# Expert phase of an attention and expert kernel: rows routed already normalised, float32r first layer, root split between ScalarE and VectorE, stores one tile later

## The chip, the cores and the metric

The kernel runs on one core of a Trainium2 chip. The metric is the device time of one execution in microseconds (us). The kernel before has a median of 1305.73 us over three executions.

## The reference

`x` is (32, 256, 128) in float32: 8192 rows of 128. The first half normalises each row, runs causal attention with 16 heads of 64 through a low-rank key and value, projects, normalises and adds `x`. The second half normalises again and sends each row to one of 8 experts:

```python
def _sublayer(xs, g, b, W1e, b1e, W2e, b2e):
    mu = jnp.mean(xs, axis=-1, keepdims=True)
    var = jnp.mean(jnp.square(xs - mu), axis=-1, keepdims=True)
    h = (xs - mu) * jax.lax.rsqrt(var + EPS) * g + b
    return xs + jax.nn.relu(h @ W1e.T + b1e) @ W2e.T + b2e
feats = x.reshape(-1, x.shape[-1])          # x is the layer-normed row
expert = jnp.argmax(feats @ centroids.T, axis=1)
alpha = jax.nn.sigmoid(jnp.sum(feats * centroids[expert], axis=-1, keepdims=True))
out = alpha * y_of_that_expert + (1.0 - alpha) * feats
x = x + _layernorm(out, axis=-1)
```

W1 is 512x128 and W2 128x512 for each expert.

## The kernel before

**Engines.** Five instruction streams are written by hand: SP (loads), PE (TensorE), ACT (ScalarE), DVE (VectorE) and POOL (GpSimd). Each runs in the order written and waits on semaphores. A value that a float32r product needs exactly is kept in two parts: `cp` on ACT makes the upper part (line 720), a subtraction on DVE the rest (for instance `z_lo`, L910), and three products (low by high, high by low, high by high) are summed.

**Attention.** 32 blocks of 256 rows, eight slots to a block, one pair of heads to a slot; `phases` runs two blocks to a trip of its loop, then a last trip, then a drain of empty slots in which only the later stages of the pipeline still work. In a slot, POOL scales the probabilities of an earlier slot (L1144, the "norm"), and beside it carries the small work of the block before: x1 = x + normalised attention (L1092, into the row buffer `pay`), its statistics' root (L1104, L1105), the normalised row `fn` (L1068), and in slot 7 two scatters of 128 rows each into the DRAM table `routed_rows` (L1135), at places that DVE's `route` works out (`dst`, L955). A row there has 136 words: x1, its reciprocal root, its shift, a second root, the best score and the row's number.

**Drain.** After the last block's counts are known (`ends`, L958), ACT and SP each store four pads of 512 rows behind the experts' regions (`pad`, L230; each needs a number read from `ends`). PE works out W1 times beta for the bias (`first_bias`, L584), and ACT scales all of W1 by gamma in place (L780), in slot 7, after the pads. The last block's row goes through st2, `an` (L829), x1, st3, `fn`, scores, `dst` and the scatter. Then DVE makes the table of tiles (to L367), and the expert phase starts.

**Expert phase.** Tiles of 256 rows of one expert; 39 can be needed, and TILES is rounded up to 40. `ffn_phases` gives every engine eight unrolled slots, a loop of eight, and an end. In slot s, tile s is loaded (SP, L246), `ff` and `nn` are made from it (DVE, L373 and L381), turned (PE, L279) and copied to `nt` (ACT, L316); ACT also copies that expert's weights, 1029 columns, from `wx` to `wst` (L308) and takes the exponential for the gate (L311), which DVE finishes (L419, L428). Tile s-1 has its first layer (PE, L263, float32) and relu (ACT L323, DVE L390), tile s-2 its second layer (PE, L289, float32) and `yt` (ACT, L330), tile s-3 is turned back (PE, L272), joined with `ff` (L408) and measured (L414, L424) on DVE, and POOL takes the root (L446, L448). Tile s-4 is normalised (DVE, `on`, L399), added to its input (POOL, `res`, L442) and stored by two indirect DMAs (POOL, L452), whose descriptors POOL makes itself. POOL's slot before:

```python
pool.wait_ge(S["on_ready"], m + 1)
g.tensor_tensor(res[:, b], on[:], fin[:, sf, :, 0:P], ALU.add)
g.tensor_tensor(gve[:], gmv[:, b3, :, 1], eps_t[:], ALU.add)
g.tensor_tensor(grs[:, b3, :], gve[:], neg_half[:], ALU.pow)
for t in range(2):
    g.indirect_dma_start(out, ...)
```

**Start.** SP loads block 0 of x, the attention weights, then the expert weights (4.1 MB), and only then block 1 of x.

## Time and profile before

| | before |
|---|---|
| median of three executions | 1305.73 us (1304.86 to 1308.39) |
| the profiled execution | 1306.78 us, span 1305.0 us |
| PE busy | 1243.9 us (95%) |
| DVE busy | 1152.1 us (88%) |
| ACT busy | 1059.5 us (81%) |
| POOL busy | 923.5 us (71%) |
| mean granted TensorE clock | 0.975 |
| chain that ended last | PE 81%, DVE 9%, issue 4%, POOL 3% |
| largest DVE groups of the expert phase in that chain | `ff` 2%, relu 1%, `on` 1%, `gg` 1% |

The span is what the trace covers; the execution's own time is 1.8 us longer. The attention fills it to about 1082 us, the drain and the table take until about 1104 us, and the rest is the expert phase. A share of the whole span hides this, so the reading goes stage by stage. "Busy" of PE counts overlapping matmuls once; the distance from one matmul's start to the next is shorter than its listed length.

### The profile page before, as it was taken

The numbers are of one execution on the slowest core, as the hardware profiler recorded it, in microseconds if no ns is written. First come the engines' busy times: TensorE is split into PE (matmuls) and PEld (weight loads), VectorE is DVE, ScalarE is ACT, GpSimd is POOL, SyncE is SP. The second block draws the span as 40 slices with busy tenths as digits, with TensorE's granted clock in tenths as the row PEclk, the third lists the DMA queues.
The fourth block names the chain that finished last, engine by engine and source line by source line (L and its number), as shares of the span: only waits on it lengthen the run. The fifth ranks groups of instructions, "written<-read, shape, count | busy, mean of one in ns | idle before, by whom it ended". The sixth has DMA issues, their size and how long they took to land.

```text
span 1305.0 us, 40537 instructions
## 1 busy us (share of the span) xinstructions
PE 1243.9 (95%) x12200; PEld 1104.5 (85%) x12200; DVE 1152.1 (88%) x4556; ACT 1059.5 (81%) x3176; POOL 923.5 (71%) x1442
## 2 busy tenths in 40 slices
PE   6999999999999999999999999999999994999992
PEld 5889888989898888888988898888888884788782
DVE  4999999999999999999999999999999884799993
ACT  4998888888888888888888888888888872566661
POOL 3567777777777777777777777777777663488886
PEclk8999999999999999999999999999999996899996
DMA  5000000000000000000000000000000003121220
GB/s 221 6 10 14 12 12 12 12 12 12 12 12 12 12 12 12 12 12 12 12 12 12 12 12 12 12 12 12 12 8 9 11 10 93 41 63 58 60 60 5
DMA packets 38505, 31.90 MB, mean 24 GB/s; under 512 B 4882, under 2 KB 35734, under 8 KB 38080
## 3 DMA queue, kind: packets, MB, share of 16 engines
q1 hardware_dynamic: 31696, 21.47, 5.4%
q0 software_dynamic: 4656, 8.81, 2.0%
q10 hardware_dynamic: 2112, 1.11, 0.3%
q8 instruction: 21, 0.34, 0.1%
q14 instruction: 20, 0.16, 0.0%
HBM read 20.35 MB, written 12.07 MB: 25 GB/s over the span
## 4 chain that ended last, share of the span: by engine, by line
PE 81%; DVE 9%; issue 4%; POOL 3%; DMA 1%; ACT 1%; SPq 0%; POOLq 0%; DVEq 0%; ACTq 0%
PE psZU L659 17%; PE psS L594 14%; PE psZU L674 14%; PE psP L626 10%; PE psZU L662 7%; PE psT L608 5%; PE psT L609 4%; PE psT L610 4%; DVE ff L373 2%; DVE wup_s L390 1%; POOL out L452 1%; DMA xin<-x 1%; DVE on L399 1%; DVE gg L408 1%; PE psS L263 1%
## 5 line engine op out<-in xcount | busy, mean ns | idle before, releaser
L1144 POOL TENSOR_TENSOR prob<-prob,rinv 128x256 f32<-128x256 f32 (+1 forms) x512 | 412.5, 827 | 254.3 <-DVE rinv L905 253.6
L756 ACT ACTIVATE prob<-nscore,nmax 128x128 f32<-128x128 f32 (+1 forms) x1024 | 453.5, 450 | 6.2 <-DVE nmax L887 5.3
L887 DVE CUSTOM_DVE_ANT_0 nscore<-psS,mask 128x128 f32<-128x128 f32 (+1 forms) x1024 | 321.5, 351 | 2.5 <-PE psS L594 1.5
L896 DVE TENSOR_TENSOR p_lo<-psP,p_hi 128x768 fp32r<-128x768 f32 x256 | 243.6, 951 | 3.0 <-ACT p_hi L720 3.0
L720 ACT ACTIVATE t_hi<-psT 128x512 fp32r<-128x512 f32 x256 | 153.0, 598 | 111.3 <-PE psT L610 108.5
L875 DVE TENSOR_TENSOR t_lo<-psT,t_hi 128x512 fp32r<-128x512 f32 x256 | 176.0, 687 | 70.5 <-ACT t_hi L720 70.1
L720 ACT ACTIVATE p_hi<-psP 128x768 fp32r<-128x768 f32 x256 | 206.7, 808 | 3.5 <-PE psP L626 3.5
L756 ACT ACTIVATION_READ_ACCUMULATOR prob<-nscore,nmax 128x1 f32 x1024 | 199.3, 195 | 0.0
L910 DVE TENSOR_TENSOR z_lo<-psZU,z_hi 128x512 fp32r<-128x512 f32 x256 | 174.1, 680 | 8.6 <-ACT z_hi L720 3.1
L594 PE MATMUL psS<-t_hi,t_lo 64*128 64x128 f32 (+1 forms) x1024 | 164.6, 317 | 0.4 <-DVE nmax L887 0.4
L608 PE MATMUL psT<-xt_hi,qk_lo 128*128 128x256 f32 x512 | 155.1, 303 | 2.3 <-DVE t_lo L875 1.2
L626 PE MATMUL psP<-ident,prob 64*128 64x64 f32 x3072 | 151.0, 231 | 0.5 <-DVE p_lo L896 0.5
L720 ACT ACTIVATE z_hi<-psZU 128x512 fp32r<-128x512 f32 x256 | 148.5, 580 | 2.1 <-PE psZU L662 2.1
L674 PE MATMUL psZU<-z_hi,b_lo 128*128 128x256 f32 x512 | 145.6, 284 | 0.0
L626 PEld LDWEIGHTS psP<-ident,prob 64*128 64x128 f32 x3072 | 116.0, 139 | 34.0 <-issue 0.7
L609 PE MATMUL psT<-xt_lo,qk_hi 128*128 128x256 f32 x512 | 143.2, 280 | 0.0
L674 PE MATMUL psZU<-z_hi,b_hi 128*128 128x256 f32 x512 | 143.2, 280 | 0.0
L594 PE MATMUL psS<-t_lo,t_hi 64*128 64x128 f32 (+1 forms) x1024 | 143.2, 275 | 0.0
L594 PE MATMUL psS<-t_hi 64*128 64x128 f32 (+1 forms) x1024 | 142.9, 275 | 0.0
L610 PE MATMUL psT<-xt_hi,qk_hi 128*128 128x256 f32 x512 | 142.9, 279 | 0.0
L674 PE MATMUL psZU<-z_lo,b_hi 128*128 128x256 f32 x512 | 142.7, 279 | 0.0
L659 PE MATMUL psZU<-p_hi,xk_lo 128*128 128x512 f32 x256 | 126.8, 495 | 1.3 <-DVE z_lo L910 1.2
(175 smaller groups left out, 3268.2 us busy)
## 6 DMA issues: line engine op xcount, KB each, us to landing
fin<-routed_rows SPq DMA_DIRECT2D x40, 136.0 KB
wx<-ffn_w SPq DMA_DIRECT2D x2, 2058.0 KB, 12.5
xin<-x SPq DMA_DIRECT2D x32, 128.0 KB, 2.2
xres<-x SPq DMA_DIRECT2D x32, 128.0 KB, 2.1
out<-res,fin POOLq DMA_INDIRECT x80
routed_rows<-padr ACTq DMA_DIRECT2D x4, 272.0 KB, 5.1
routed_rows<-padr SPq DMA_DIRECT2D x4, 272.0 KB, 4.4
wup_s<-wup SPq DMA_DIRECT2D x1, 1024.0 KB, 5.8
```

The source lines that it names most:

```text
L594: last = mm(psS[:, e, a:z], qq[h, tb, 0, q * P:(q + 1) * P], kk[h, tb, 1, 0:z - a], start=(n == 0), stop=(n == 2))
L608: mm(psT[:, m, :], qk_lo[:, r, m, :], xt_hi[:, db, :], start=True, stop=False)
L609: mm(psT[:, m, :], qk_hi[:, r, m, :], xt_lo[:, db, :], start=False, stop=False)
L610: last = mm(psT[:, m, :], qk_hi[:, r, m, :], xt_hi[:, db, :], start=False, stop=True)
L626: last = nc.tensor.transpose(psP[:, e, 64 * n:64 * n + 64], prob[half, s % 4, h, k * P:(k + 1) * P], ident[half, half])
L659: mm(psZ[:, :, :], xx[:, zx, 0, :], pp[:, zb, :, 0:T], start=(n == 0), stop=False, skip_group_check=True)
L674: last = mm(psU[:, 0:T], bb[:, hh, :], zz[:, ub, h, :], start=(ur == 0 and h == 0 and n == 0), stop=(ur == PAIRS - 1 and h == 1 and n == 2))
L720: cp = lambda o, i: nc.scalar.activation(o, i, ACT.Copy)
L756: last = nc.scalar.activation(prob[:, pb, h, a:z], nscore[:, (s - lag) % 2, h, a:z], ACT.Exp, bias=nmax[:, pb, h, q:q + 1], scale=-1.0, ac ...
L887: last = v.tensor_tensor_reduce(nscore[:, n1, h, a:z], psS[:, h, a:z], mask[:, a:z], -1.0, -MASKED, ALU.add, ALU.min, nmax[:, p1, h, q:q + 1])
L896: v.tensor_tensor(by_half(p_lo, s % 2), psPh, by_half(p_hi, s % 2).bitcast(F32), ALU.subtract).then_inc(S["p_split"], 1)
L1144: last = g.tensor_tensor(pr, pr, rinv[:, p2, :, q:q + 1].broadcast_to([P, 2, z - a]), ALU.mult)
```

## The change

- The routed row has 260 words: the row normalised twice (128), x1 (128), the gain alpha times the second root, the second root squared times EPS, and the number. POOL and DVE make these in the attention's slots (POOL slots 4, 5 and 7; ACT and DVE slot 6 take exponential, sum and reciprocal for alpha). The scatter goes behind the norm in slot 7. The expert phase no longer makes `ff`, `nn` and alpha.
- W1 scaled by gamma is made in two parts in a buffer of its own, one expert in each of the drain's slots 1 to 8: ACT the upper part, DVE the rest. The eight scalings at the end are gone.
- The first layer is three float32r products per block of 128 (12 in place of 4 float32 ones, each of which is two instructions); `nt` has an upper part (ACT) and a rest (DVE). ACT copies the weights as 1024 and 517 columns.
- The second root: ACT takes Sqrt of two single columns with the row's own EPS as bias, DVE the reciprocal. POOL's two operations go; it copies the two row numbers instead.
- `gg` moves to s-4, `on` and `res` to s-5, the stores to s-6, behind `res` of the following tile; the load of a tile waits for `res` and not for the stores. TILES is 39, and buffers are shared with the attention's.
- SP loads block 1 of x ahead of the expert weights.

```diff
-    TILES += -TILES % 8
-        sp.wait_ge(stored[s], n0 + n0)
+        sp.wait_ge(S["res_ready"], m0 + s - 7)
+        sp.wait_ge(S["ids_ready"], m0 + s - 7)
 # PE, slot s
-        last = mm(psH[:, j, :], wst[:, (s - 1) % 4, j * P:(j + 1) * P], nt[:, (s - 1) % 2, :],
-                  start=True, stop=True)
+        for n, (m, nt) in enumerate(((1, nt_hi), (0, nt_lo), (0, nt_hi))):
+            last = mm(psH[:, j, :], w1st[:, b, m, j * P:(j + 1) * P], nt[:, b, :],
+                      start=(n == 0), stop=(n == 2))
 # ACT, slot s (new order: yt, root, first weights, relu, nt, second weights)
+        act.wait_ge(S["gmv_ready"], m0 + s - 4)
+        for t in range(2):
+            last = nc.scalar.activation(gsd[:, b, t:t + 1], gmv[:, b, t, 1:2], ACT.Sqrt,
+                                        bias=fin[:, sf, t, C_EPS:C_EPS + 1])
 # DVE, end of slot s
+        v.reciprocal(grs[:, b, :], gsd[:, b, :])
+        last = v.tensor_scalar(on[:, b, t, :], gg[:, b, t, :], gmv[:, b, t, 0:1], grs[:, b, t:t + 1], ...)
+        v.tensor_tensor(nt_lo[:, s % 2, :], psN[:, 0:T], nt_hi[:, s % 2, :].bitcast(F32), ALU.subtract)
 # POOL, slot s
-        g.tensor_tensor(gve[:], gmv[:, b3, :, 1], eps_t[:], ALU.add).then_inc(S["gve_done"], 1)
-        g.tensor_tensor(grs[:, b3, :], gve[:], neg_half[:], ALU.pow).then_inc(S["grs_ready"], 1)
+        g.tensor_copy(ids[:, c, :], fin[:, sf, :, C_ID].bitcast(U32)).then_inc(S["ids_ready"], 1)
 # ACT, attention's slots
+    if not live(0) and 1 <= s <= E:
+        nc.scalar.activation(w1[:, s - 1, 0, :], wx[:, s - 1, 0:FB * P], ACT.Copy, scale=gam[:, s - 1:s])
-    if not live(0) and s == 7:
-        act.wait_ge(S["bias_done"], E // 2 + 1)
-        for e in range(E):
-            last = nc.scalar.activation(wx[:, e, 0:FB * P], wx[:, e, 0:FB * P], ACT.Copy,
-                                        scale=gam[:, e:e + 1])
 # DVE, head of a slot
+    if not live(0) and 1 <= s <= E:
+        dve.wait_ge(S["w1_hi_done"], s)
+        v.scalar_tensor_tensor(w1[:, s - 1, 1, :], wx[:, s - 1, 0:FB * P], gam[:, s - 1:s],
+                               w1[:, s - 1, 0, :].bitcast(F32), ALU.mult, ALU.subtract)
 # DVE, end of slot 6
+    v.tensor_scalar(ea1[:], ea[:], 1.0, None, ALU.add)
+    v.reciprocal(alpha[:], ea1[:])
 # POOL, slot 4
+    g.tensor_tensor(pay[:, db, :, 0:P], fn[:], rstd2[:].unsqueeze(2).broadcast_to([P, 2, P]), ALU.mult)
 # SP, start
+    sp.wait_ge(S["x_loaded"], 16)
+    load_x(xin, 1, 1, S["x_loaded"])
     for dst_, src in ((cent[:], cent_t), ..., (wx[:, E // 2:], ffn_w[:, E // 2:])):
```

ACT in the drain, before: from the copy `at` of the last block to the exponential of the first tile.

```order
L720 ACTIVATE at<-psZU 128x256
L229 TENSOR_LOAD ends
L229 ISA x2
L230 ISA
L230 DMA routed_rows<-padr 128x4x136
...
L230 DMA routed_rows<-padr 128x4x136
L780 ACTIVATE wx<-wx,gam 128x512 x8
L720 ACTIVATE ft<-psM 128x256
```

The same place of the change (`w` is the new buffer of scaled W1, `best` the best score).

```order
L764 ACTIVATE w<-wx,gam 128x512 x2
L721 ACTIVATE at<-psZU 128x256
L781 ACTIVATE ea<-best 128x2
...
L237 DMA routed_rows<-padr 128x4x260
L764 ACTIVATE w<-wx,gam 128x512 x2
L721 ACTIVATE ft<-psM 128x256
```

Two of the eight scalings, experts 6 and 7, stand behind ACT's four pads. DVE at the same place of the change, from the destination of the block before the last to the statistics of the last block's x1:

```order
L955 TENSOR_REDUCE dst<-dsel 128x2
L958 CAST ends<-base 128x8
L1002 TENSOR_SCALAR ea<-ea 128x2
L1004 RECIPROCAL alpha<-ea 128x2
L964 SCALAR_TENSOR_TENSOR w<-wx,gam,w 128x512
L819 BN_STATS st<-psM 128x6 x2
L825 BN_AGGR mv<-st 128x2 x2
L964 SCALAR_TENSOR_TENSOR w<-wx,gam,w 128x512
L830 TENSOR_SCALAR an<-psM,mv,rs 128x128 x2
L971 TENSOR_TENSOR wx<-psT,wx 128x8x4
L819 BN_STATS st<-pay 128x6 x2
```

Before, `st<-psM` (L818) followed `ends` directly; now the rest of W1 for expert 6 stands between them. POOL in the expert phase's loop, before and then in the change (`wq_s` is where `res` now lies, `xres` where `on` lies, `softmax` where `fin` lies):

```order
L442 TENSOR_TENSOR res<-on,fin 128x256
L445 REGISTER_ALU
L446 TENSOR_TENSOR gve<-gmv,eps_t 128x2
L448 TENSOR_TENSOR grs<-gve,neg_half 128x2
L452 DMA out<-res,fin 8192x128 x2
```

```order
L446 TENSOR_TENSOR wq_s<-xres,softmax 128x256
L447 COPY ids<-softmax 128x2
L453 DMA out<-wq_s,ids 8192x128 x2
```

The root has left POOL; the stores that follow `res` are those of the tile before.

## Rows read from the trace of the kernel before

**Rows 1.** Busy time by window, attention: length, then PE, PEld, DVE, ACT, POOL, clock, DMA, GB/s.

```profile
600.00:604.00 4.00, 4.00 (x52) 3.60 (x50) 3.74 (x16) 3.47 (x11) 3.50 (x5) 1.00 0.05 17
```

**Rows 2.** Busy time by window, expert phase.

```profile
1140.00:1256.00 116.00, 112.32 (x549) 92.96 (x548) 112.80 (x469) 75.13 (x164) 99.33 (x139) 1.00 0.21 61
```

**Rows 3.** Timeline, one tile of the expert phase: start us, length us, engine, line.

```profile
1198.83 1.89 PE L263 MATMUL psS<-nt,wst 128*128 128x256 f32 x8
1201.03 0.20 PEld L279 LDWEIGHTS psZU<-ident,nn 128*128 128x128 f32 x2 [0.33 <-DVE nn L381]
...
1201.68 0.64 DVE L399 TENSOR_SCALAR on<-gg,gmv,grs 128x128 f32<-128x128 f32 x2
...
1202.59 0.97 POOL L452 DMA_INDIRECT out<-res,fin  x1 [0.30 <-DVE on L399]
...
1203.04 1.89 PE L263 MATMUL psS<-nt,wst 128*128 128x256 f32 x8
1203.23 0.46 DVE L419 TENSOR_SCALAR ea<-ea 128x2 f32<-128x2 f32 x1
...
1203.57 0.74 POOL L442 TENSOR_TENSOR res<-on,fin 128x256 f32<-128x256 f32 x1
...
1205.45 1.03 POOL L452 DMA_INDIRECT out<-res,fin  x1 [0.19 <-issue]
```

**Rows 4.** Chain of waits: start, length, what; matmuls as issued one behind another.

```profile
1118.25 1.73 PE psT L289 x8
```

**Rows 5.** Chain of waits, drain: float32r matmuls.

```profile
1073.21 0.71 PE psZU L674 x6
```

**Rows 6.** Groups by line, 1080 to 1305 us: busy us, mean ns, then idle before.

```profile
L308 ACT ACTIVATE wst<-wx 128x1029 f32 x40 | 42.5, 1063 | 21.8 <-issue 12.6 <-DVE table L367 8.4 <-ACT yt L330 0.8
...
L311 ACT ACTIVATE ea<-fin 128x2 f32<-128x2 f32 x40 | 7.6, 189 | 1.5 <-DMA fin<-routed_rows 1.5
```

**Rows 7.** Timeline, DVE before POOL has any store to issue.

```profile
1107.38 0.16 DVE L419 TENSOR_SCALAR ea<-ea 128x2 f32<-128x2 f32 x1
```

**Rows 8.** Timeline, start of the kernel.

```profile
0.78 1.28 ACT L720 ACT_TABLE_LOAD   x1 [0.65 <-PEq L1181]
...
20.79 0.49 DVE L818 BATCH_NORM_STATS2 st<-xin 128x6 f32<-128x128 f32 x2 [2.21 <-DMA xin<-x]
```

**Rows 9.** Timeline, attention, end of slot 6 on DVE and POOL.

```profile
632.01 0.66 DVE L910 TENSOR_TENSOR z_lo<-psZU,z_hi 128x512 fp32r<-128x512 f32 x1
...
632.18 1.61 POOL L1144 TENSOR_TENSOR prob<-prob,rinv 128x256 f32<-128x256 f32 x2 [0.69 <-DVE rinv L905]
```

**Rows 10.** Chain of waits, the following slot's product on PE.

```profile
633.85 0.90 PE psZU L659 x3
```

**Rows 11.** Timeline, drain, from the pads to the last block's destination.

```profile
1084.35 5.21 ACTq L230 DMA_DIRECT2D routed_rows<-padr  x4
...
1086.49 0.21 POOL L1011 TENSOR_TENSOR ve<-mv,eps_t 128x2 f32<-128x2 f32 x1
...
1088.41 0.72 POOL L1092 TENSOR_TENSOR pay<-an,xres 128x256 f32<-128x256 f32 x1 [0.84 <-DVE an L829]
...
1090.12 5.01 ACT L780 ACTIVATE wx<-wx,gam 128x512 f32<-128x512 f32 x8 [7.64 <-PE psT L584]
1090.23 0.47 DVE L818 BATCH_NORM_STATS2 st<-pay 128x6 f32<-128x128 f32 x2
...
1092.29 1.58 POOL L1068 TENSOR_SCALAR fn<-pay,mv 128x128 f32<-128x128 f32 x2 [0.19 <-POOL pay L1105]
...
1098.38 0.17 DVE L955 TENSOR_REDUCE dst<-dsel 128x2 uint32<-128x16 f32 x1
```

**Rows 12.** Timeline, expert phase: the first tile's first layer, the last tile's, the last store.

```profile
1108.69 3.78 PE L263 MATMUL psS<-nt,wst 128*128 128x256 f32 x8 [0.47 <-ACT nt L316]
...
1275.36 1.89 PE L263 MATMUL psS<-nt,wst 128*128 128x256 f32 x8
...
1295.75 0.97 POOL L452 DMA_INDIRECT out<-res,fin  x1 [0.30 <-issue]
```

319 lines of the change are left out of this document (171 added, 148 removed).

## The prediction, made before the changed kernel ran

> **What bounds the kernel now.** I read the busy time by window first, because the page's shares mix stages. In the attention PE is busy for 4.00 of 4.00 us [rows 1] and DVE for 3.74: PE is the bound, and what ACT, DVE or POOL gain or lose there costs nothing as long as PE's inputs stay early. In the expert phase PE is busy 112.3 of 116 us, DVE 112.8, POOL 99.3, ACT 75.1 [rows 2]. These hardly differ, so I went to the timeline of one tile [rows 3]. First layer to first layer is 1203.04 - 1198.83 = 4.21 us. In it PE waits 0.33 us for `nn`. Its own work is two layers of 1.73 us each [rows 4] and two pairs of transposes; these fill 4.21 - 0.33 - 3.46 = 0.42 us. So PE works 3.88 and idles 0.33. POOL has hardly a gap: `res` begins at 1203.57, the next store at 1205.45, so `res` and the root take 1.88 us; then come 1.03 us for the first store, a gap of 0.30 and 0.97 for the second, 4.18 together. POOL and PE meet at nearly the same period, with DVE between them. One can not gain without the others.
>
> **The start.** DVE waits 2.21 us for block 1 of x [rows 8], which stands in SP's queue behind 4.1 MB of expert weights, and everything after it in DVE's queue waits too, then POOL, then PE. Ahead of those weights the load is early. The weights are needed only in the drain, a thousand us later. Gain 2.2 us; bounds 1 and 3.5 (the next waiter may be 1 us behind; or PE loses less speed while it waits).
>
> **Attention.** Per block POOL gets a 128x256 product of about 0.75 us (like `res` [rows 3]) and four operations of about 0.2, and loses one; ACT one small Exp; DVE one addition (0.16 [rows 7]) and one reciprocal of about that. POOL's scatter now stands behind the norm. The place to check is the end of DVE's slot 6: `z_lo` ends at 632.67 [rows 9] and the product that needs it starts at 633.85 [rows 10], 1.18 us later. 0.3 us of DVE fit. I take 0; bounds 0 and the second rival.
>
> **The drain.** It looks as if 5.01 us of scaling by ACT left the path [rows 11]. They do little there: `ft` waits for them until about 1095.0 (1090.12 and 5.01, less an overlap of 0.1), and `fn`, its other input, starts at 1092.29 and with 1.58 us and the transposes would have let it start at 1094.6. Gain 0.4. What is added is worse. Two of the new scalings stand behind ACT's four pads, whose issue lasts from 1084.35 to 1089.56, and DVE takes the rest of W1 ahead of the last block's statistics. Forward: the DVE operations ahead of `dst` and `ends` move the pads by 0.5, to 1090.1. ACT's scaling 0.7 (5.01 / 8 and its end), to 1090.8. DVE's rest, a 128x512 operation like `z_lo` (0.66 [rows 9]), to 1091.5; statistics 0.5 and their aggregation 0.3, to 1092.3. From POOL's root to the end of x1 it takes 1089.13 - 1086.49 = 2.64, to 1095.0. The statistics of x1 now start at 1095.05, before at 1090.23 (where they waited for the bias, which PE finishes long before now). From there `fn` comes 2.06 later as before, and `dst` too: 4.8 late, less the 0.4 of `ft`, 4.4. Behind it the order is a little longer: the gain needs DVE's reciprocal after `dst`, a POOL product, then the scatter; and the table starts 0.3 later. About 0.4 of this shows in the first load. The pads carry 1040 bytes a row in place of 544, so they last longer, but they end near 1100 and the last scatter comes at 1104. The first tile's load carries twice the bytes (+0.3); it sheds `ff` and `nn` (-1.2) and gets `nt_lo` and a semaphore (+0.6). Sum: 4.4 + 0.4 - 0.3 = **+4.5 us** at the first product. Bounds +2 (if the two scalings get ahead of the pads' numbers) and +7 (if every link has a gap more).
>
> **A tile of the expert phase.** PE: six float32r products take 0.71 us [rows 5], so twelve take 1.42 where the float32 layer took 1.73; PE works 3.88 - 0.31 = 3.57. POOL loses the root and gets a copy of about 0.2: `res` 0.74, copy 0.2, gap 0.2, stores 2.30, that is 3.44. DVE loses four passes of 128x128 (two pairs like `on`, 0.64 each, a little less), the addition with its hold (0.46) and gets `nt_lo`, half of a `z_lo` with a fixed part, 0.42: 4.09 (112.8 over 27.6 tiles) - 1.2 - 0.46 + 0.42 + 0.1 = 2.95. ACT gets longer: 75.1 over 27.6 is 2.72; less the Exp 0.19, plus 512 columns more at 1.06 for 1029 [rows 6], 0.53, plus a fixed 0.1, plus two Sqrt like that Exp, 0.38: 3.54. The root is no longer a chain of POOL's, but ACT and DVE pass it to and fro; it has a whole slot for each step.
>
> So PE, ACT and POOL stand at 3.57, 3.54 and 3.44: no engine can wait long for another. The ring that closes each tile is first layer, relu, `nt` upper part, `nt` rest, first layer: 1.42, three ACT operations of 256 columns (two relus and the copy to `nt`; each below the 0.53 of 512 columns [rows 6], together 1.2 to 1.5) and 0.42, with four semaphores 3.2 to 3.5, and DVE has the reciprocal and `on` (0.64) between relu and `nt_lo`. It fits below 3.57 only when `on` isn't held. Today's interlock costs PE 0.33; I leave that as it is: **3.90 us** a tile. Bounds 3.57 (PE alone) and 4.15 (first rival).
>
> Does a store hold `on`? The small DVE addition takes 0.16 alone [rows 7] and 0.46 when it starts at 1203.23 inside a store; it ends with that store [rows 3]. So DVE is held by a store's later part. But `on` at 1201.68 took 0.64 for its pair inside the store before it, the twin of the one at 1205.45, with hardly any hold. The Trainium skill, SBUF — State Buffer, section Who interferes with whom, says that whoever issues first keeps the shared ports for the whole instruction and the other is blocked fully. By that rule `on` would wait for each store's end, which the addition bears out and `on` does not; this is the first rival, with its price from the rows.
>
> From the first tile's first layer to the last's the trace shows 1275.36 - 1108.69 = 166.7 us [rows 12] for 39 steps: 39 x 4.21 = 164.2 and 2.5 for slow first tiles. Now 38 steps (39 tiles): 38 x 3.90 = 148.2, the same 2.5, and one load of the table for Sqrt, 1.3 by the load of 1.28 at the start [rows 8]: 152.0. **-14.7 us**, of which 4.2 are the tile left out. The Trainium skill, ScalarE: Activation LUTs, section What ACT_TABLE_LOAD costs, adds a drain of 1.38 us to each load; the sum would be 1.4 worse by it, and no row here shows that drain.
>
> **The end.** From the last tile's first layer to the end of the last store it takes 1296.72 - 1275.36 = 21.4 us, at POOL's pace. The new lag is longer by a slot for `yt` and one for the stores; about six pairs of stores are left, 6 x 3.44 = 20.6, and some 2 of phase: 22.6. **+1.2**; bounds -1 and +3.
>
> **Sum.** -2.2 + 0 + 4.5 - 14.7 + 1.2 = -11.2 us. From the profiled execution's 1306.8 us that is 1295.6; that execution is 1.05 us above the median of the three shown, and against the median of 1305.73 it is **1294.5 us**.
>
> **Rivals.**
> 1. *The stores hold `on`.* Then `on` waits for the second store, `res` for `on`, and the next stores for `res`: 0.60 + 0.74 + 0.2 + 0.2 + 1.03 + 0.30 + 0.97 and 0.1 for semaphores, 4.15 us a tile. 38 x 0.25 = 9.5 more: 1304.0. For it speaks the held addition, against it the free `on`. A partial hold gives 4.05 and 1300.
> 2. *Slower: the new addition in DVE's slot 6 is held by the norm.* It stands right behind the reciprocal that releases POOL's norm of 1.61 us [rows 9]. If it starts after the norm, it waits for its end: 1.61 and 0.15, against the 1.18 us that `z_lo` has in hand, so PE stands still for 0.6 us in each of 31 blocks: +18, 1312.5. It decides from a hold of 1.5 us on: 0.5 a block costs the whole gain and 0.3% more. Against it: the norm starts at 632.18, after `z_lo` at 632.01, so the addition, in `z_lo`'s place, is first.
> 3. *The drain does not lengthen, or the tiles run at 3.7.* If ACT and DVE get the last scalings done in the shadow of other work, 4.5 falls to 0: 1290. At 3.7 us a tile it is 1287.
> 4. *The period stays at 4.2*, since ACT's copies come late for the relus: only the tile and the start are won, -2.2 + 4.5 - 2.9 + 1.2, so 1306.
>
> **How the numbers follow.** My forecast with periods between 3.75 and 4.0 (1289 to 1298.5) gets 0.53, the first rival 0.20, the second 0.06, the third 0.14, the fourth 0.07. A measurement of this kernel can tell about 0.3%, 3.9 us: below 1301.8 is faster. There lie the forecast, the third and half of the first, 0.77. The other half, the fourth and a little of the second are no change, 0.17; slower 0.06. The range, 1287 to 1303.5, leaves out the second and fourth rival and the worst of the first.
>
> **What would show it.** Right: no DVE wait for x at 20 us; first layer to first layer about 3.9 us; ACT and PE both near full in the phase, POOL waiting for `on`; the statistics of the last x1 near 1095 less the 2.2 won at the start, waiting behind the rest of W1 and so behind ACT's pads; one table load. Wrong: `on` pairs of 1 us or more that end with a store (first rival); PE waits for `z_lo` once a block (second); ACT without gaps and PE waiting for relu (fourth); statistics of x1 that start where they did (third).

## The result, and the profile after

The changed kernel is slower: 1346.65 us median of four runs (1345.34 to 1352.24) against 1307.06 us for the kernel before beside it, ratio 1.031, 95% interval 1.029 to 1.034. The forecast was 1294.5 us in a range of 1287 to 1303.5, so both the number and the side are wrong. The profiled execution took 1352.24 us with a span of 1348.0 us, 43.0 more than the span before. Cut at the same places in both timelines (first product of block 1 and of block 30, the first and the last tile's first layer):

| stretch | before, us | after, us | difference | forecast |
|---|---|---|---|---|
| to block 1 | 47.45 | 43.98 | -3.5 | -2.2 |
| block 1 to block 30 (29 blocks) | 948.2 | 982.5 | **+34.3** | 0 |
| block 30 to the first tile's first layer | 113.05 | 130.8 | **+17.8** | +4.5 |
| first tile to last tile | 166.7 | 160.0 | **-6.7** | -14.7 |
| last tile's first layer to the end of the span | 29.6 | 30.7 | +1.1 | +1.2 |

(The forecast counted the end to the end of the last store: 22.5 us against 21.4, +1.2.) Three terms failed: the attention, which I had costed at nothing, the drain, and the tiles.

**The attention.** The waits of 100 to 1000 us of the kernel after (engine, what it was about to write, line, releaser: us in total, times, longest). The last four lines shown have no counterpart of any size in the kernel before (the first of them has 2.2 us there, the others are not in its list):

```profile
...
ACT t_hi L721 <- PE psT L611: 101.0, 185, 0.9
DVE t_lo L876 <- ACT t_hi L721: 44.0, 106, 0.7
PEld psZU L660 <- issue: 38.2, 27, 1.5
DVE an L830 <- POOL rs L1024: 37.7, 27, 1.4
PE psZU L660 <- DVE z_lo L911: 33.5, 27, 1.3
ACT softmax L757 <- DVE nmax L888: 22.6, 26, 1.0
...
```

27 times in 900 us, at 33.9 us a block, is once a block. The timeline of one block, POOL, then DVE, then PE (start, length, engine, line, what, and in brackets the idle time before it):

```profile
619.05 1.61 POOL L1155 TENSOR_TENSOR softmax<-softmax,rinv 128x256 f32<-128x256 f32 x2 [2.27 <-DVE rinv L906]
620.84 1.12 POOL L1170 DMA_INDIRECT routed_rows<-pay,dst  x1 [0.17 <-issue]
622.26 0.96 POOL L1170 DMA_INDIRECT routed_rows<-pay,dst  x1 [0.30 <-issue]
623.25 0.21 POOL L1022 TENSOR_TENSOR ve<-mv,eps_t 128x2 f32<-128x2 f32 x1
623.53 0.72 POOL L1024 TENSOR_TENSOR rs<-ve,neg_half 128x2 f32<-128x2 f32 x1
...
624.29 0.73 DVE L830 TENSOR_SCALAR an<-psM,mv,rs 128x128 f32<-128x128 f32 x2 [1.40 <-POOL rs L1024]
624.94 0.68 DVE L911 TENSOR_TENSOR z_lo<-psZU,z_hi 128x512 fp32r<-128x512 f32 x1
...
625.77 0.47 PE L660 MATMUL psZU<-p_both,xk_lo 128*128 128x512 f32 x1 [1.24 <-DVE z_lo L911]
```

Read it upwards. PE waits 1.24 us for `z_lo`; `z_lo` stands in DVE's queue behind `an`, which waits 1.40 us for the root `rs`; and the root stands in POOL's queue behind the two scatters, which with their gaps take from 620.66 to 623.22. Ahead of its norm POOL now sits idle for 2.27 us: into that gap the scatter used to fall. The product that waits is that of [rows 10].

**The drain.** Timeline after, from `ends` to the last x1:

```profile
1127.25 0.16 DVE L958 CAST ends<-base 128x8 int32<-128x8 f32 x1
...
1133.61 1.33 ACT L764 ACTIVATE w<-wx,gam 128x512 fp32r<-128x512 f32 x2 [7.21 <-issue]
1134.37 0.75 DVE L964 SCALAR_TENSOR_TENSOR w<-wx,gam,w 128x512 fp32r<-128x512 f32 x1 [6.68 <-ACT w L764]
1135.04 0.49 DVE L819 BATCH_NORM_STATS2 st<-psM 128x6 f32<-128x128 f32 x2
...
1138.96 0.49 DVE L819 BATCH_NORM_STATS2 st<-pay 128x6 f32<-128x128 f32 x2 [0.74 <-POOL pay L1104]
```

Here the forecast holds: DVE waits 6.68 us for the two scalings that stand behind ACT's pads. From `ends` to the statistics of the last x1 it takes 11.7 us. Before it took 7.0, from the line below to 1090.23 [rows 11]:

```profile
1083.22 0.16 DVE L958 CAST ends<-base 128x8 int32<-128x8 f32 x1
```

So this part is 4.7 longer, where I had worked out 4.3 (4.8 for the statistics, of which 0.5 was the later `ends`). The other 13.2 us lie ahead of `ends`, where I had put 0.5.

**The tiles.** First and last first layer and the last store:

```profile
1157.27 0.58 PE L274 MATMUL psS<-xt_hi,p_both 128*128 128x256 f32 x1 [0.93 <-DVE xt_lo L432]
...
1317.27 0.39 PE L274 MATMUL psS<-xt_hi,p_both 128*128 128x256 f32 x1
...
1338.81 0.98 POOL L453 DMA_INDIRECT out<-wq_s,ids  x1 [0.30 <-issue]
```

160.0 us for 38 steps are 4.21 us a step, the pace of the kernel before [rows 3, 12] and not 3.90. The waits of 1185 to 1300 us:

```profile
PEld psS L274 <- DVE xt_lo L432: 17.2, 24, 1.4
...
PE psS L274 <- DVE xt_lo L432: 10.2, 15, 1.0
ACT xt_hi L345 <- PE psZU L290: 9.7, 12, 1.0
ACT wup_s L340 <- PE psS L274: 7.8, 12, 1.2
DVE xt_lo L432 <- ACT xt_hi L345: 6.7, 10, 0.7
```

(`xt_hi`, `xt_lo` are `nt_hi`, `nt_lo` here.) In the first experiment below, with the very same code in this phase, the third and the fifth of these lines are gone and the second is down to 0.7 us.

### The profile page after: what moved, and what is told of

It is laid out like the page before. It is cut to its first block, busy times and chain, and to the rows that moved or that the text cites. A ratio compares the mean times of both kernels' runs of the same rounds, so it can differ in the third digit from the quotient of the medians.

```text
span 1348.0 us, 40987 instructions
## 1 busy us (share of the span) xinstructions
PE 1234.4 (92%) x12336; PEld 1102.3 (82%) x12336; DVE 1132.3 (84%) x4455; ACT 1087.3 (81%) x3281; POOL 924.9 (69%) x1495
## 4 chain that ended last, share of the span: by engine, by line
PE 68%; issue 11%; POOL 9%; DVE 6%; DMA 2%; ACT 1%; ACTq 0%; POOLq 0%; DVEq 0%; SPq 0%
PE psZU L660 14%; PE psS L595 11%; PE psZU L675 11%; PE psP L627 8%; PE psZU L663 5%; PE psT L609 4%; PE psT L610 4%; PE psT L611 3%; PE psS L274 3%; POOL routed_rows L1170 3%; POOL softmax L1155 2%; POOL out L453 2%; DVE z_lo L911 2%; DMA xin<-x 1%; DVE softmax L888 1%
## 5 line engine op out<-in xcount | busy, mean ns | idle before, releaser
L1155 POOL TENSOR_TENSOR softmax<-softmax,rinv 128x256 f32<-128x256 f32 (+1 forms) x512 | 412.8, 827 | 257.0 <-DVE rinv L906 257.0
L757 ACT ACTIVATE softmax<-softmax,nmax 128x128 f32<-128x128 f32 (+1 forms) x1024 | 453.8, 450 | 31.9 <-DVE nmax L888 30.8
L888 DVE CUSTOM_DVE_ANT_0 softmax<-psS,mask 128x128 f32<-128x128 f32 (+1 forms) x1024 | 322.4, 353 | 4.9 <-issue 2.6
L897 DVE TENSOR_TENSOR p_both<-psP,p_both 128x768 fp32r<-128x768 f32 x256 | 243.9, 953 | 4.8 <-ACT p_both L721 4.8
L721 ACT ACTIVATE p_both<-psP 128x768 fp32r<-128x768 f32 x256 | 206.7, 807 | 5.3 <-PE psP L627 5.3
L757 ACT ACTIVATION_READ_ACCUMULATOR softmax<-softmax,nmax 128x1 f32 x1024 | 199.5, 195 | 0.0
L660 PE MATMUL psZU<-p_both,xk_lo 128*128 128x512 f32 x256 | 127.3, 497 | 40.0 <-DVE z_lo L911 40.0
L660 PE MATMUL psZU<-p_both,xk_hi 128*128 128x512 f32 x512 | 161.8, 397 | 0.0
L627 PE MATMUL psP<-ident,softmax 64*128 64x64 f32 x3072 | 151.8, 232 | 0.5 <-DVE p_both L897 0.5
L627 PEld LDWEIGHTS psP<-ident,softmax 64*128 64x128 f32 x3072 | 116.6, 139 | 34.3 <-issue 0.9
```

The lines of the kernel that those rows point to most:

```text
L627: last = nc.tensor.transpose(psP[:, e, 64 * n:64 * n + 64], prob[half, s % 4, h, k * P:(k + 1) * P], ident[half, half])
L660: mm(psZ[:, :, :], xx[:, zx, 0, :], pp[:, zb, :, 0:T], start=(n == 0), stop=False, skip_group_check=True)
L721: cp = lambda o, i: nc.scalar.activation(o, i, ACT.Copy)
L757: last = nc.scalar.activation(prob[:, pb, h, a:z], nscore[:, (s - lag) % 2, h, a:z], ACT.Exp, bias=nmax[:, pb, h, q:q + 1], scale=-1.0, ac ...
L888: last = v.tensor_tensor_reduce(nscore[:, n1, h, a:z], psS[:, h, a:z], mask[:, a:z], -1.0, -MASKED, ALU.add, ALU.min, nmax[:, p1, h, q:q + 1])
L897: v.tensor_tensor(by_half(p_lo, s % 2), psPh, by_half(p_hi, s % 2).bitcast(F32), ALU.subtract).then_inc(S["p_split"], 1)
```

## The experiments

Each is told by its edit against the kernel named. Experiments 1 to 4 ran together on one chip, and so did 5 to 8, 9 to 11, 12 to 14, and 15 and 16, each group on another chip and with the kernel before beside it. This matters for the pace of the tiles, as the part behind experiment 16 shows. "A step" is the mean distance of the tiles' first layers, first to last, over 38 steps.

**1. The scatter ahead of the norm.** The changed kernel with one block moved in POOL's slot 7:

```diff
                     g.tensor_tensor(pay[:, db, :, C_GAIN], rstd2[:], alpha[:], ALU.mult).then_inc(S["gain_ready"], 1)
+                if r == 7 and live_b(2):
...
+                    for t in range(2):
+                        g.indirect_dma_start(rows, bass.IndirectOffsetOnAxis(ap=dst[:, db, t:t + 1], axis=0),
+                                             pay[:, db, t, :], None).then_inc(S["rows_written"], 16)
                 if live(2):
...
-                if r == 7 and live_b(2):
...
-                    for t in range(2):
-                        g.indirect_dma_start(rows, bass.IndirectOffsetOnAxis(ap=dst[:, db, t:t + 1], axis=0),
-                                             pay[:, db, t, :], None).then_inc(S["rows_written"], 16)
```

> The changed kernel with one move: in POOL's slot 7 the scatter of the routed rows stands ahead of the norm again (behind the product that makes the gain), as in the kernel before; all else stays. Theory A (the place of the scatter): behind the norm it stands directly ahead of the root that DVE's `an` waits for, `z_lo` is queued behind `an`, and PE waits about 1.27 us in each steady block; with the move the block period falls from 34.00 us back to 32.7, some 27 blocks, and the stalls of 2.7 us at the start of the drain go too: the kernel comes to 1302 to 1312 us, 35 to 45 less than the changed kernel's 1346.65, and `an <- POOL rs` vanishes from the waits. Theory B (the operations that POOL, ACT and DVE gained in the attention are what is late, wherever the scatter stands): the period stays above 33.5 us and the kernel above 1335. Theory C (both): the period falls by part, 1318 to 1330.

Measured: 1297.14 us (1294.87 to 1299.3, four runs), ratio to before 0.992 (0.990 to 0.995), so 49.5 us less than the changed kernel. `an <- POOL rs` is gone from the waits, and 29 blocks take 947.5 us (before 948.2). POOL in one block:

```profile
597.19 1.12 POOL L1160 DMA_INDIRECT routed_rows<-pay,dst  x1 [0.97 <-POOL pay L1148]
598.61 0.96 POOL L1160 DMA_INDIRECT routed_rows<-pay,dst  x1 [0.30 <-issue]
599.59 1.62 POOL L1168 TENSOR_TENSOR softmax<-softmax,rinv 128x256 f32<-128x256 f32 x2
...
601.43 0.72 POOL L1024 TENSOR_TENSOR rs<-ve,neg_half 128x2 f32<-128x2 f32 x1
```

The root follows the norm at once; POOL's queue holds the same work, in another order. Theory A holds. That the gain is above the expected 35 to 45 comes from the tiles: a step takes 3.89 us, not 4.21, with not a line changed there, which is 12.2 us of the 49.5. Those 12.2 are not shown to be the scatter's: the two kernels ran on different chips.

**2. The kernel before with the scatter behind the norm.** The same move in the old kernel, nothing added:

```diff
-                if r == 7 and live_b(2):
...
-                        g.indirect_dma_start(rows, bass.IndirectOffsetOnAxis(ap=dst[:, db, t:t + 1], axis=0),
-                                             pay[:, db, t, :], None).then_inc(S["rows_written"], 16)
                 if live(2):
...
                     prep_rstd(b0 + db + 3)
+                if r == 7 and live_b(2):
...
+                        g.indirect_dma_start(rows, bass.IndirectOffsetOnAxis(ap=dst[:, db, t:t + 1], axis=0),
+                                             pay[:, db, t, :], None).then_inc(S["rows_written"], 16)
```

> The kernel before with that one move the other way: the scatter of slot 7 stands behind the norm and the preparation, ahead of the next slot's root; no operation is added. Theory A: 27 blocks x 1.27 us and the stall at the drain's start are added, 1340 to 1350 us. Theory B (the added operations): nothing happens, 1305 to 1309. Theory C (the scatter costs only together with the added operations of POOL): in between, 1315 to 1330.

Measured: 1347.79 us (1344.45 to 1353.55), ratio 1.033 (1.030 to 1.036). The move alone costs 41 us. It shows the same waits, `DVE an L829 <- POOL rs L1013: 35.9, 26, 1.4` among them. 29 blocks take 981.7 us (+33.5), and from block 30 to the first tile 119.4 us (+6.3). Since experiment 1 has all the added operations and the old length of a block, they cost nothing that shows; B and C fall.

**3. The scalings of W1 earlier as well.**

```diff
+        W1_AT = ((0, 1), (2,), (3,), (4, 5), (6,), (7,))
...
-                if not live(0) and 1 <= s <= E:
+                if not live(0) and s < 6:
                     act.wait_ge(S["ffnw_loaded"], 5 * 16)
-                    nc.scalar.activation(w1[:, s - 1, 0, :], wx[:, s - 1, 0:FB * P], ACT.Copy,
-                                         scale=gam[:, s - 1:s]).then_inc(S["w1_hi_done"], 1)
+                    for e in W1_AT[s]:
+                        nc.scalar.activation(w1[:, e, 0, :], wx[:, e, 0:FB * P], ACT.Copy,
+                                             scale=gam[:, e:e + 1]).then_inc(S["w1_hi_done"], 1)
...
-                if not live(0) and 1 <= s <= E:
+                if not live(0) and 1 <= s < 7:
+                    for e in W1_AT[s - 1]:
```

(The last two lines are DVE's, whose rests follow one slot later.)

> The kernel of the move above (scatter ahead of the norm) and a second edit: ACT scales the eight experts' W1 in the drain's slots 0 to 5 (two, one, one, two, one, one) in place of 1 to 8, DVE takes the rests one slot later, so that no scaling stands behind ACT's pads and no rest ahead of the last block's statistics waits for them. Theory (the prediction's drain term): the statistics of the last x1 come some 4.8 us earlier and the first tile with them: 4 to 5.5 us less than the run with the scatter alone. Rival (the drain is longer for another reason: the low clock of a PE that was held, or the longer order of scatter, pads and loads): 0 to 1 us less; or the two more scalings per slot make ACT late for PE in the drain's first slots: 1 to 3 us more.

Measured: 1289.82 us (1289.08 to 1294.53), ratio 0.988 (0.986 to 0.991), 7.3 us less than experiment 1. From `ends` to the last statistics it takes 7.2 us again (4.5 less). The rest was got ahead of `ends`: 94.6 us from block 30 in experiment 1, 90.7 here, 87.6 before. The windows show what differs there: PE's busy time and the granted clock (ninth number, the one before DMA's share), experiment 1, then experiment 3.

```profile
1061.00:1065.00 4.00, 2.31 (x24) 1.88 (x23) 3.58 (x11) 3.34 (x11) 3.92 (x6) 0.96 0.01 3
1065.00:1069.00 4.00, 4.00 (x28) 3.98 (x26) 2.57 (x8) 1.21 (x2) 2.70 (x5) 0.50 0.11 33
1069.00:1073.00 4.00, 4.00 (x23) 3.59 (x21) 1.66 (x3) 2.02 (x3) 3.50 (x9) 0.50 0.00 0
1073.00:1077.00 4.00, 4.00 (x24) 3.58 (x25) 1.50 (x2) 0.81 (x1) 1.23 (x5) 0.50 0.01 4
```

```profile
1062.00:1066.00 4.00, 2.37 (x25) 2.00 (x24) 3.66 (x12) 4.00 (x14) 3.90 (x6) 1.00 0.06 23
1066.00:1070.00 4.00, 3.49 (x34) 3.19 (x33) 4.00 (x8) 2.67 (x7) 2.30 (x3) 1.00 0.11 33
1070.00:1074.00 4.00, 4.00 (x40) 3.75 (x39) 3.29 (x7) 2.75 (x5) 2.91 (x7) 1.00 0.00 0
```

In the first, PE stands still for part of 4 us in the drain's second slot and then runs some 12 us at half its clock (1.2 GHz) with its queue full. In the other it pauses at least as long, but the clock stays at 1.00. In the changed kernel PE is busy 2.45 and 1.54 us in two such windows (1100 to 1108), and then the clock is 0.50 from 1108 to 1120 us. In its repeat (experiment 5) PE is busy 2.25 and 1.56 us in the same windows, and the clock is then 0.76 for 4 us and 1.00 for the next 8; `ends` comes 3.9 us sooner behind block 30. So the low clock goes with some 3.9 us, and it can differ between two executions of one kernel: the 3.9 us that experiment 3 gains ahead of `ends` are not shown to be the edit's, although all four executions of it have a higher mean clock (0.974 to 0.978) than those of experiment 1 (0.970 to 0.972).

**4. The early load of x alone.**

```diff
             sp.dma_start(wo_s[:], wo).then_inc(S["o_loaded"], 16)
+            sp.wait_ge(S["x_loaded"], 16)
+            load_x(xin, 1, 1, S["x_loaded"])
...
-            sp.wait_ge(S["x_loaded"], 16)
-            load_x(xin, 1, 1, S["x_loaded"])
```

> The kernel before with only the load of block 1 of x ahead of the expert weights. Theory: the whole gain of 3.5 us that the changed kernel shows up to the start of block 1 (first product of block 1 at 43.98 us in place of 47.45) comes from this: 3.3 to 3.7 us less, about 1303.4 us. Rival: it brings the 2.2 us of DVE's wait as predicted, and the rest is owed to another edit: 1304.8.

Measured: 1302.0 us, in a single execution. Block 1 starts at 42.55 us; block 0 itself takes 30.3 us from its first product on, as in the changed kernel, and 34.1 before. (The first product comes between 11.2 and 13.7 us in the different executions, so the block's own length is the better measure: -3.8.) The whole gain at the start is the load's.

**5. The changed kernel again.** From here on the question is the pace of the tiles.

> The changed kernel once more, unchanged, on the chip of the next runs. Its expert phase ran at 4.21 us a tile, and the same phase, behind the attention with the scatter moved, at 3.82; nothing in the phase differs between the two. Theory P (two paces: the phase settles into one or the other by the moment at which loads, stores and transposes meet, and the moment is set by what runs ahead of it): the pace is again 4.2, or it is 3.8 in this execution, and then the times of this kernel fall into two groups some 12 us apart, about 1340 and 1347 to 1352. Theory Q (the slow pace belongs to the kernel, through the order on POOL): 4.21 in the profile again, times 1345 to 1352. Theory R (one disturbed execution): 3.82 in the profile, times about 1346 as they were.

Measured: 1345.6 us (1344.2 to 1346.29), ratio 1.030 (1.028 to 1.032), a step 4.18 us; from block 30 to `ends` 96.9 us in this execution, against 100.8 in the first. The slow pace is repeated. R falls; so does P's second group of times.

**6. Half the bytes in each load.** The row's layout becomes normalised values, gain, eps, number, x:

```diff
-                sp.dma_start(fin[:, s], rows[bass.ds(row, T), :].rearrange("(t p) c -> p t c", p=P)
+                sp.dma_start(fin[:, s, :, 0:C_X], rows[bass.ds(row, T), 0:C_X].rearrange("(t p) c -> p t c", p=P)
```

> The changed kernel with the row laid out as normalised values, gain, eps, number, and x behind them, and the load of a tile brings only the first 132 of the 260 columns: 528 bytes a row in place of 1040. It leaves out the residual x of the expert phase (what is added is what the buffer held). Theory L (the burst of the tile's load delays the transposes that read the same memory, or their signal): with half the bytes the pace falls from 4.21 to 3.8 or less, some 12 to 15 us less than the changed kernel in the same job. Rival (the pace has nothing to do with the load): 4.2 stays, or it is 3.8 in all runs of this job.

Measured: 1342.17 us, a step 4.12 us beside 4.18 in experiment 5. Theory L falls: the bytes are not it.

**7. The scalings early, scatter still behind.** The edit of experiment 3 on the changed kernel.

> The changed kernel, its scatter still behind the norm, with only the scalings of W1 moved to the drain's slots 0 to 5. Theory for the drain: 5 to 7 us less than the changed kernel up to the first tile, as the same edit brought with the scatter ahead. For the pace of the tiles: theory P says either value, theory Q 4.2.

Measured: 1342.78 us, 2.8 less than experiment 5. From `ends` to the last statistics 6.7 us against 11.7, the first tile 4.1 us earlier; the stretch ahead of `ends` stays as it was (96.4 us), since `an` still waits there. The gain is a little under what was expected. A step takes 4.19 us.

**8. No root on ACT.** Experiment 3 with one word changed:

```diff
-                        last = nc.scalar.activation(gsd[:, b, t:t + 1], gmv[:, b, t, 1:2], ACT.Sqrt,
+                        last = nc.scalar.activation(gsd[:, b, t:t + 1], gmv[:, b, t, 1:2], ACT.Identity,
```

> The kernel with the scatter ahead and the scalings early, and ACT's root of the variance replaced by a plain Identity with the same bias: it leaves out the root of the second normalisation in the expert phase (it divides by the variance). What it tests: the execution's time is 4.2 to 4.5 us above the span of its profile in the kernels with the change, and 1.8 to 1.9 in those without it. Theory T (the table of functions: the program ends with another table than it begins with): without Sqrt it is 1.8 again, and one load of the table of 1.3 us goes from the phase: 1289.8 falls by 2.4 plus at most 1.3, to 1286.1 to 1287.4. Rival (what lies around the span belongs to the larger program or its buffers): 4.3 stays, and the kernel gains at most 1.3 us.

Measured: 1307.34 us with a span of 1302.8 us, so 4.5 us still lie around the span: theory T falls. What I did not expect is that the kernel with less to do is 17 us slower than the one it was made from. Of these, 11 lie between the first and the last tile: a step takes 4.19 us instead of 3.89. The other 6 lie ahead of the first tile, where the two kernels are the same, 4.9 of them in the 29 blocks (952.6 us against 947.7). The slow pace is therefore not tied to the scatter: a kernel with the scatter ahead has it too. Nor is it shown to be tied to the root that is left out, since the time that is lost where nothing was changed points at where the kernel ran.

**9. SP issues each load 0.3 us later**, on experiment 3 (`wait_apart(sp, S["h_done"], m0 + s - 2)` ahead of the load):

> The kernel with the scatter ahead and the scalings early (1289.8 us, 3.81 us a tile), with one wait more on SP: from the ninth tile on, the load of a tile is issued only when PE's first layer of the slot is done, 0.3 us later than it was and so right where PE's transposes end and POOL issues its second store. Theory I (moment of issue): in the runs with the slow pace ACT starts the copy of the transposed tile up to 1 us late whenever SP's issue and POOL's second issue start together, while in the fast ones SP's issue stands 0.6 us ahead of POOL's second. So here the pace becomes 4.1 to 4.25 us, the phase 159 in place of 147.9, the kernel 1300 to 1303. Rival (the pace hangs on something else, such as the moment at which the bytes arrive, which this shifts by 0.3 us only): 3.8 stays and 1290.

**10. SP issues each load a good 2 us later**, on the changed kernel (the same line with `S["yt_done"], m0 + s - 3`):

> The changed kernel (4.18 to 4.21 us a tile) with one wait more on SP: from the ninth tile on, the load is issued only when the second layer of the next slot's end is done (the tile four ahead of the load's), which is some 0.2 us into a first layer and 0.5 us ahead of POOL's first store. Theory I: the issue now never meets POOL's second store or the transposes, the pace falls to 3.7 to 3.8 us, and the phase from 159 to 144 to 148: 1345.6 becomes 1331 to 1335. Rival (POOL's stores alone delay what PE signals, or the slow pace is carried by the rhythm of the engines): 4.1 to 4.2 stays, 1343 or more.

Measured: 1306.95 us and 4.20 us a step in experiment 9, as theory I said; but 1342.17 us and 4.09 us a step in experiment 10, where it had said 3.7 to 3.8. There SP's issue stood alone, and ACT waited for PE's transposes all the same. Theory I falls as a cause: moving SP's issue does not take the slow pace away. That it brought the pace on in experiment 9 is not shown, since experiment 3 ran on another chip, and experiment 9 too takes 952.5 us for the 29 blocks, in which its loads play no part.

**11. A load of one row**, issued at the same moment, on the changed kernel:

```diff
+                if live(FU):
+                    sp.dma_start(fin[0:1, s, 0, :], rows[bass.ds(row, 1), :]).then_inc(f_loaded[s], 16)
+                else:
```

> The changed kernel in which the load of each tile from the ninth on brings one row of 1040 bytes in place of 256 rows, issued at the same moment. It leaves out the data of all tiles but the first eight. It tells the issue from the bytes: theory I in its narrow form (the moment alone at which SP issues a transfer, whatever its size) keeps 4.1 to 4.2 us. Theory I in its wide form (the 256 descriptors or the bytes of the load that meet those of the store) gives 3.7 to 3.8 and 1331 to 1335. Half the bytes in the same 256 rows had kept 4.12, so the bytes alone speak for little.

Measured: 1345.72 us, a step 4.18 us. One row of 1040 bytes in place of 256 changes nothing: experiment 10, beside it on the same chip, has 4.09.

**12 to 14. One store, no load, no store**, each on the changed kernel.

```diff
-                    for t in range(2):
+                    for t in range(1):
```

> The changed kernel in which POOL stores only the first half of each tile: the second indirect DMA of each slot, which POOL issued where PE's transposes end, is left out (rows 128 to 255 of each tile are not stored). Theory J (POOL's issue of the second store is what delays ACT's start behind PE's transposes): the phase goes from 4.17 to 3.7 us a tile or less, 1346 to 1328 to 1333. Rival (the delay comes from something else): 4.1 to 4.2 stays.

```diff
-                if not live(0):
+                if not live(0) or live(FU):
                     return
...
+                    if not live(FU):
                         pe.wait_ge(f_loaded[s], n0 + 16)
```

> The changed kernel in which SP issues no load from the ninth tile on and PE waits for none (all later tiles compute on the data of the first eight). SP is silent in the phase. Theory K (SP's reading of the table and its issue, whatever the size of the load, are needed for the slow pace): 3.7 to 3.8 us a tile and 1330 to 1334. Rival J (POOL's stores alone): 4.1 to 4.2 stays. The load of one single row had kept 4.17, which leaves the issue itself open.

```diff
+                    late = isinstance(m0, int) and m0 + s - 6 >= 26
-                    for t in range(2):
+                    for t in range(2 if late else 0):
```

> The changed kernel in which POOL stores only the last 13 tiles (the first 26 are left out of the output). With SP's loads as they are and no store in the first 26 tiles, theory J says 3.6 to 3.7 us a tile there, and the slow pace, if any, only behind. Theory K and theories in which PE's, ACT's and DVE's own rhythm makes the slow pace say 4.1 to 4.2 in the first 26 tiles as well.

Measured: 1328.16, 1334.1 and 1333.91 us; a step 3.85, 3.84 and 3.88 us. All three run at the fast pace. The waits of 1185 to 1285 us with one row a load (experiment 11; the lines are 3 lower there), then with one store (experiment 12):

```profile
PEld psS L277 <- DVE xt_lo L435: 15.3, 22, 1.4
...
ACT xt_hi L348 <- PE psZU L293: 9.2, 14, 1.0
```

```profile
POOL wq_s L446 <- DVE xres L427: 48.7, 27, 2.7
...
PEld psS L274 <- DVE xt_lo L432: 7.3, 24, 0.8
```

ACT's wait for PE's transposes is in the first and not in the second. It is tempting to read that POOL's two stores and SP's loads must both be there for the slow pace. The runs do not show it: the changed kernel itself was not run beside these three, and the times of experiments 13 and 14 are near what it would take at the fast pace (an estimate: its 1346.65 less the 12.2 us by which the tiles of experiment 1 are shorter is 1334.4). Experiment 12 is lower, and why was not looked into. Experiments 1 and 3 have all the stores and all the loads and are fast.

**15. The scalings in slots 2 to 5**, none in 0 and 1, on experiment 3.

> The kernel with the scatter ahead and the scalings early, but ACT scales two experts in each of the drain's slots 2, 3, 4 and 5 and none in 0 and 1, where PE still has full work: there, in the runs before, PE was busy 2.3 of 4 us and in one of them its clock then fell to 1.2 GHz. Theory (ACT's scalings in slots 0 and 1 hold the copies that PE waits for): the destination of the last block comes up to 3 us earlier, as early as in the kernel before, and the kernel takes 1286 to 1288 against 1289.8. Rival (the gap is the end of the first layers' work and has nothing to do with the scalings, or eight scalings in four slots hold the ranking instead): 0 to 2 us more. For the pace of the tiles, 3.8 or 4.2, only that it is one of the two: at 4.2 it would be some 12 us more.

Measured: 1290.68 us (1290.21 to 1292.06), ratio 0.988 (0.986 to 0.989): no better. `ends` comes 91.5 us behind block 30, against 90.7. PE is busy for only 2.29 of 4 us from 1062 to 1066, so its pause at the start of the drain is not made by the scalings.

**16. Experiment 3 again.**

> The kernel with the scatter ahead and the scalings early once more, unchanged. Theory P' (the pace of the tiles is fixed by the kernel's own timing): 3.81 us a tile again and 1289 to 1294 us in all runs. Theory P'' (the pace falls either way from one execution to the next): some runs at 1301 to 1304, or 4.1 to 4.2 in the profile.

Measured: 1291.85 us (1289.66 to 1293.18), ratio 0.988 (0.987 to 0.990), a step 3.85 us. Experiments 5 and 16 each repeat the pace of their kernel, but both in the kind of profile that their kernel had at first, as the next part shows.

**In every run the pace goes with the group in which the kernel ran.** The groups (on which chip the result was taken is not on record), the step of the tiles, and whether the profile records the landing (the arrival) of POOL's indirect transfers:

| ran together | us a step | landings of POOL's transfers |
|---|---|---|
| the result (changed kernel) | 4.21 | not in the profile |
| experiments 1, 3 | 3.89, 3.89 | recorded |
| experiments 5, 6, 7, 8 | 4.18, 4.12, 4.19, 4.19 | not in the profile |
| experiments 9, 10, 11 | 4.20, 4.09, 4.18 | not in the profile |
| experiments 12, 13, 14 | 3.85, 3.84, 3.88 | recorded |
| experiments 15, 16 | 3.89, 3.85 | recorded |

No group has both paces, and no kernel with the change was run in groups of both. The mark is there long before the tiles, in code that is the same. Experiments 3 and 8 have one attention; this is one block of each, POOL's second scatter, the transposes of the probabilities on PE, and ACT's copy of them, first in experiment 8, then in experiment 3:

```profile
600.53 0.96 POOL L1163 DMA_INDIRECT routed_rows<-pay,dst  x1 [0.30 <-issue]
600.63 0.59 PE L628 MATMUL psP<-ident,softmax 64*128 64x64 f32 x12
602.17 0.81 ACT L722 ACTIVATE p_both<-psP 128x768 fp32r<-128x768 f32 x1 [0.76 <-PE psP L628]
```

```profile
630.99 0.96 POOL L1163 DMA_INDIRECT routed_rows<-pay,dst  x1 [0.30 <-issue]
631.07 0.59 PE L628 MATMUL psP<-ident,softmax 64*128 64x64 f32 x12
631.75 0.81 ACT L722 ACTIVATE p_both<-psP 128x768 fp32r<-128x768 f32 x1
```

The copy starts 0.95 us after the transposes' listed end in the one and 0.09 in the other. Over the 27 blocks from 100 to 980 us it is 0.78 to 0.98 us in experiments 8 and 9, and 0.09 to 0.15 in 1, 3, 15 and 16. It is the same picture as in the slow tiles, with POOL's indirect transfer beside the transposes, and in experiment 8 SP issues no load within 4 us of any of these late copies. So the comparisons across groups (8 and 9 with 3, 12 to 14 with 5 and 11, and the tiles of 1 with those of the changed kernel) say nothing of what the edits do to the pace. The comparisons within a group stand, and so does the attention: experiment 2 ran in the group of experiment 1 and takes 981.7 us for the 29 blocks against 947.5.

## Why the prediction was wrong, step by step

- **Attention, 0 forecast, +34.3 measured: the step that failed.** It stood in one sentence, "POOL's scatter now stands behind the norm", and the next named the end of DVE's slot 6 as the place to check. That is where the new DVE operation stands, not where the scatter went. The scatter's place is POOL's slot 7, and behind it comes the next slot's root; `an` waits for that root, and `z_lo` of the slot stands behind `an`. The sum was there to be made from rows of any block: two issues of 1.12 and 0.96 us and their gaps are 2.56 us on POOL, moved out of an idle stretch of 2.27 us ahead of the norm into the busy stretch between norm and root. 1.24 of the 2.56 us come through to PE in a block; over 29 blocks it is 34.3, 1.18 each. Experiments 1 and 2 show it from both sides: -35.0 and +33.5 us in the 29 blocks.
- **The slower rival** had the right form (something held ahead of `z_lo`, once a block, PE idle) and the wrong cause: it named the addition held by the norm. No row of after shows the addition held: it takes 135 to 140 ns in each of 27 blocks.
- **Start, -2.2 forecast.** The load is the cause, and the wait of 2.21 us is gone. It brought -3.5 (-3.8 in experiment 4): the bound of 3.5 that I had named.
- **Drain, +4.5 forecast, +17.8 measured.** The two scalings behind the pads cost 4.7 for the 4.3 worked out, and the steps behind them came out as before to 0.2 us. The term that was mis-sized is the one ahead of the pads, "move the pads by 0.5": 7.0 us in experiment 1, 13.2 in the changed kernel and 9.3 in its repeat. I had priced DVE's and ACT's operations, and neither the late `z_lo` in the last blocks nor what a PE that is held can pay after: slots at half the clock, which go with 3.9 of the 13.2. How the rest divides was not measured.
- **Tiles, 3.90 forecast, 4.21 measured.** Experiments 1, 3, 15 and 16 give 3.85 to 3.89 over the whole phase, start and table load included, and most single steps 3.70 (1162.72 to 1166.42 us in experiment 1). The phase is then bound by PE, as the sum of 3.57 said, with 0.13 in place of the 0.33 that I kept from the old interlock. So the sum of the engines was right (-18.9 us in experiment 1 against -14.7), and the changed kernel misses it through a wait that no sum of busy times shows. The fourth rival had named the period of 4.2, for another reason: ACT without gaps and late for the relus. ACT has gaps (9.7 us ahead of `xt_hi`, 7.8 ahead of the relus); it waits for PE.
- **The stores do not hold `on`** (first rival): its operations take 352 ns each in the changed kernel, and the 49 of 78 that have a store under way beside them take 347. The Trainium skill's rule of an exclusive lock on the shared ports (SBUF — State Buffer, Who interferes with whom), which it gives for DVE instructions in a two-port mode, would have had `on` wait for each store's end if it runs in such a mode, which no row tells. No such wait is in the trace.
- **The table load.** Experiments 3 and 8 differ by it in the fifth step: 5.09 us with it (1123.69 to 1128.78; 5.08 or 5.09 at either pace) and 3.76 without (1130.07 to 1133.83), 1.33 us for this load (timeline of experiment 3):

```profile
1124.55 1.28 ACT L324 ACT_TABLE_LOAD   x1
```

  The drain of 1.38 us that the Trainium skill adds (ScalarE: Activation LUTs, What ACT_TABLE_LOAD costs) does not show in the step.
- **The end** came out at +1.2 for +1.2, by the last store.

With the scatter put back, the forecast's terms stand at: start -4.6, attention -0.7, drain +11.5, tiles -18.9, end +1.0, together -11.7 us of span against -11.2 forecast, and 1297.1 us. That this is near 1294.5 is in part luck: the drain and the tiles were both off, in opposite directions. It is also the sum at the fast pace alone. The result was taken at the slow one, where the scatter ahead was run only in experiments 8 and 9: 1307 us, no better than the kernel before.

**What stays open** is what makes the two paces. One step of each pace, ACT only, first of the changed kernel, then of experiment 1:

```profile
1197.52 0.82 ACT L340 ACTIVATE wup_s<-psS,w2st 128x256 f32<-128x256 f32 x2
1199.33 0.38 ACT L345 ACTIVATE xt_hi<-psZU 128x256 fp32r<-128x256 f32 x1 [0.98 <-PE psZU L290]
```

```profile
1164.62 0.82 ACT L340 ACTIVATE wup_s<-psS,w2st 128x256 f32<-128x256 f32 x2
1165.33 0.38 ACT L345 ACTIVATE xt_hi<-psZU 128x256 fp32r<-128x256 f32 x1
```

and PE in the same two steps:

```profile
1197.45 0.38 PE L290 MATMUL psZU<-ident,softmax 128*128 128x128 f32 x2
1197.67 1.89 PE L301 MATMUL psT<-wup_s,w2st 128*128 128x256 f32 x8
```

```profile
1164.47 0.38 PE L290 MATMUL psZU<-ident,softmax 128*128 128x128 f32 x2
...
```

From the start of the transposes to ACT's copy it takes 1.88 us in the one and 0.86 in the other. In the first the copy begins 1.5 us after the transposes are listed as ended (1197.83), though the matmuls behind them run on. So either their real end or their signal is late. The Trainium skill (Perfetto Trace Analysis, Tensor Engine Instruction) says that the profiler computes a matmul's end from its size and that the signal goes out only when PSUM has acknowledged the bytes; no run here can tell the two apart. Shown is that the late step comes and goes with the group of runs (the table above), that a late copy stands beside POOL's indirect transfers in the attention too, and that where it is there, it does not hang on the bytes or rows of SP's loads (6, 11) nor on SP's moment (10). Whether it goes away without the stores or the loads is not shown, since experiments 12 to 14 ran where a kernel with both is fast as well. What differs between the two kinds of group, and whether it is the chip, was not found. No run has the changed kernel and experiment 3 side by side in one group, which would separate the kernel from the place. Open too is why 4.2 to 4.6 us lie around the span in the changed kernels and 1.8 or 1.9 in the old: it is 1.8 where fewer stores are issued (experiments 12 and 14; 4.3 in 13 beside them) and 4.5 without Sqrt (8).

**The version that beats both** is experiment 3: 1289.8 and 1291.9 us on two chips, 1.2% under the kernel before, both at the fast pace. At the slow pace it was not run; experiments 8 and 9, which differ from it in one word and one wait, took 1307.34 and 1306.95 us there, beside 1306.94 and 1306.85 for the kernel before. So the gain may be nothing on such a chip.

## What to carry to other kernels

When an instruction moves, look at its new place: list what stands behind it in its own queue, who waits for that, and what stands behind the waiter on the next engine, until an engine is reached that has no time in hand. An issue that fills an idle gap is free, and the same issue on the other side of a norm need not be (here 1.24 of its 2.56 us came through to PE in each block); the test is to move it alone, in the old kernel, before anything is built on it. And where a phase has an interlock of five engines, a sum of busy times gives the best pace, not the one that it falls into. Before an edit is credited with a change of pace, run both kernels side by side, and look at a stretch that the edit does not touch: if that has changed too (here 952.6 us for 947.7), the edit is not shown to be the reason.
